# A graph-attention layer and a masked attention layer on 64 graphs: a software pipeline five steps deep replaced by one of twelve steps

## The reference, cut

```python
h = jnp.maximum(_layernorm(x), 0.0)
xl = (h @ W1).reshape(B, N, 4, 128)
e = leaky_relu(asrc[:, :, None, :] + adst[:, None, :, :], 0.2)     # asrc, adst: xl times att_src, att_dst
attn = softmax(where(mask, e, -1e9), axis=1)
h = elu(einsum('bsdh,bshf->bdhf', attn, xl) + b1)
x = x + gat_layer(h, W2, ...)                                      # the same with one head
h = jnp.maximum(_layernorm(x), 0.0)
scores = where(adj, einsum('bhnd,bhmd->bhnm', h @ Wq, h @ Wk) / sqrt(32), -inf)
x = x + relu(einsum('bhnm,bhmd->bhnd', softmax(scores), h @ Wv)) @ Wo
```

## Time and profile before

| | us |
|---|---|
| median of 3 runs | 1104.64 (1102.05 to 1110.62) |
| the profiled execution, its time | 1103.94 |
| its span, first to last instruction | 1102.4 |
| mean granted TensorE clock in it | 0.924 of full speed |
| busy in the span: TensorE, VectorE, ScalarE, GpSimd | 877, 680, 604, 517 |

### The profile page before, as it was taken

How to read it: one execution, slowest core, us unless ns; L and a number is a source line. 1 busy time by engine, 2 the same in 40 slices (tenths; PEclk the granted TensorE clock), 3 DMA queues, 4 the chain that set the end, 5 groups by cost and what they waited for, 6 DMA issues and landing times.

```text
span 1102.4 us, 25604 instructions
## 1 busy us (share of the span) xinstructions
PE 877.0 (80%) x8776; PEld 672.6 (61%) x8776; DVE 680.0 (62%) x2015; ACT 603.7 (55%) x1865; POOL 517.1 (47%) x733
## 2 busy tenths in 40 slices
PE   1277888888888888888888888888888888888884
PEld 0155666666666666666666666666666666666652
DVE  5245667666766666666666666666666666666652
ACT  0245566556666565656555565556565565656541
POOL 3334455445544554455445544544454454445422
PEclk9587999899999998999899899989998998999885
DMA  5001223233322332133122323322431333222122
GB/s 147 0 9 32 58 64 63 38 58 63 64 46 50 64 64 53 42 63 64 42 55 63 59 42 58 64 53 42 64 63 37 59 63 51 45 64 63 38 36 53
DMA packets 165967, 59.45 MB, mean 54 GB/s; under 512 B 138448, under 2 KB 165456, under 8 KB 165840
## 3 DMA queue, kind: packets, MB, share of 16 engines
q1 hardware_dynamic: 165840, 57.83, 27.2%
HBM read 15.86 MB, written 8.39 MB: 22 GB/s over the span
## 4 chain that ended last, share of the span: by engine, by line
PE 59%; DVE 23%; issue 8%; ACT 5%; DMA 2%; POOL 2%; SPq 1%; DVEq 0%; POOLq 0%; ACTq 0%
PE bank L693 21%; PE bank L707 10%; PE bank L832 8%; DVE top L641 7%; PE bank L788 5%; DVE qkT L612 4%; ACT qkT L410 3%; DVE att L587 2%; PE bank L778 2%; DVE x L625 2%; DVE hT L519 2%; PE bank L824 2%; PE bank L719 2%; DMA e3T<-e_split 1%; PE bank L733 1%
## 5 line engine op out<-in xcount | busy, mean ns | idle before, releaser
L319 POOL TENSOR_TENSOR rstd<-var,minus_half 128x1 f32<-128x1 f32 x128 | 71.4, 558 | 300.1 <-DVE var L537 293.2
L420 ACT ACTIVATE e<-bank,nmx,q_power 128x128 f32<-128x128 f32 x512 | 192.6, 471 | 0.0
L307 POOL TENSOR_TENSOR e_split<-e,e_split 128x512 f16<-128x512 f32 x128 | 148.1, 1157 | 10.3
L641 DVE TENSOR_REDUCE top<-bank 128x8 f32<-128x1024 f32 x64 | 78.3, 1224 | 88.3 <-PE bank L788 88.3
L707 PE MATMUL bank<-w,h1T 128*128 128x258 f32 x512 | 127.1, 391 | 0.7 <-DVE h1T L557 0.7
L358 ACT ACTIVATE lr<-bank,power 128x512 f32<-128x512 f32 x64 | 44.0, 688 | 139.3 <-PE bank L744 139.3
L693 PE MATMUL bank<-w_split,hT 128*128 128x260 f16 x768 | 103.5, 288 | 18.2 <-DVE w_split L487 14.7
L297 POOL TENSOR_TENSOR eTn<-eT,rs 128x512 f32<-128x512 f32 x64 | 66.5, 1040 | 108.6 <-DVE rs L637 108.6
L832 PE MATMUL bank<-en,xl 128*128 128x128 f32 x512 | 97.8, 351 | 20.3 <-DVE x L625 18.3
L371 ACT ACTIVATE eT<-lr,nmx 128x128 f32<-128x128 f32 x256 | 98.9, 394 | 18.3 <-DVE nmx L602 18.3
L832 PEld LDWEIGHTS bank<-en,xl 128*128 128x128 f32 x512 | 84.2, 249 | 35.3 <-issue 31.4
(11 more groups left out here) (118 smaller groups left out, 2047.1 us busy)
## 6 DMA issues: line engine op xcount, KB each, us to landing
x_in<-in_x_dram SPq DMA_DIRECT2D x64, 128.0 KB, 2.4
out_dram<-x_out SPq DMA_DIRECT2D x64, 128.0 KB, 1.7
adj_in<-in_adj_dram SPq DMA_DIRECT2D x64, 64.0 KB, 2.1
e3T<-e_split SPq DMA_TRANSPOSE x128, 3.1
w<-in_L_gnn_W_dram SPq DMA_DIRECT2D x2, 256.0 KB, 3.1
w<-in_L_gnn_W_dram SPq DMA_DIRECT2D x1, 512.0 KB, 6.5
att<-in_L_gnn_att_src_dram SPq DMA_DIRECT2D x1, 256.0 KB, 5.1
att<-in_L_gnn_att_dst_dram SPq DMA_DIRECT2D x1, 256.0 KB, 5.7
```

The costliest lines, as they stand in the source:

```text
L307: pool.tensor_tensor(e3_split[:, g.two, half, 1], e, e3_split[:, g.two, half, 0], ALU.subtract).then_inc(s[low_set], 1)
L319: pool.tensor_tensor(rstd[:, g.two, which:which + 1], var[:, g.two, which:which + 1], minus_half[:, :], ALU.pow).then_inc(s[rstd_set], 1)
L420: ins = act.activation(e3[:, g.two, h, :], S[:, h // 4, (h % 4) * N:(h % 4 + 1) * N], ACT.Exp, bias=nmx3[:, g.two, h:h + 1], scale=q_power ...
L641: dve.tensor_reduce(top3[:, g.two, :], S.rearrange("p b (h n) -> p (b h) n", h=4), AX.X, ALU.max, negate=True).then_inc(s["top3_set"], 1)
```

## The change

Every function becomes an item of its own with a lag of 0 to 11 in place of a phase, so that a graph is spread over twelve steps and a full step has twelve graphs in flight; 75 steps do the 64 graphs. Nearly every function keeps its instructions. What is new:
- the order of the items on all five engines, and the lags;
- the eight banks are dealt out anew: Z (bank 7) and Z2 (bank 6) share with S; ABT, O1, T3 and WO share bank 0; ET and AV bank 1; T1, ET2 and O2 bank 3; XL, V, T2 and QK banks 4 and 5; X2 has bank 2 alone;
- x_in, x1 and the masks have rings of eight; load is split in load_adj (lag 2) and load_x (lag 0), and only x of graph 0 is loaded ahead of the weights;
- the mask matmul of scores1, that of scores3, the variance of both norms, ab_high, ab_low, and ab2_evac are items of their own; the sums of W2 run at the first project2;
- `after` and `at_ends` are waits for the readers of a bank: `after` in every step, `at_ends` in the first and last twelve graphs only;
- the preparation of the weights moves from steps 1 to 4 to steps 5 to 8.

The diff, cut to its core:

```diff
-P_, A_, B_, C_, D_ = range(5)
-L_ = -1
+LAGS = 12
...
+def after(eng, sem, g, lag):
+
+    wait(eng, sem, min(g.n + lag + 1, g.count))
+
+
+def at_ends(eng, sem, g, lag):
+
+    if g.n < LAGS or g.n >= g.count - LAGS:
+        after(eng, sem, g, lag)
...
+        x_in = sb("x_in", [128, 8, D])
...
+        mask_gat = sb("mask_gat", [128, 8, N], BF16)
+        mask_mha = sb("mask_mha", [128, 8, N], BF16)
...
-        XL, X2, AV, Z2, Z = bank[:, 0:2, :], bank[:, 4], bank[:, 5], bank[:, 6], bank[:, 7]
-        QK, ET2, T3, V, O2, S = bank[:, 0], bank[:, 4], bank[:, 5], bank[:, 1], bank[:, 6], bank[:, 2:4, :]
-        ABT = bank[:, 5, 0:N // 2].bitcast(F16)
-        T2, ET, WO, T1, O1 = bank[:, 7], bank[:, 7], bank[:, 5], bank[:, 0], bank[:, 6]
+        XL = bank[:, 4:6, :]
+        T1 = bank[:, 3]
+        ABT = bank[:, 0, 0:N // 2].bitcast(F16)
+        Z = bank[:, 7]
+        ET = bank[:, 1]
+        O1 = bank[:, 0]
+        X2 = bank[:, 2]
+        Z2 = bank[:, 6]
+        ET2 = bank[:, 3]
+        O2 = bank[:, 3]
+        T2 = bank[:, 5]
+        QK = bank[:, 5]
+        V = bank[:, 4]
+        S = bank[:, 6:8, :]
+        AV = bank[:, 1]
+        T3 = bank[:, 0]
+        WO = bank[:, 0]
...
-            def load(g):
-                free(sp, s["x1_set"], g, 4)
-                sp.dma_start(x_in[:, g.four, :], x[g.n]).then_inc(x_here[g.four], 16)
+            def load_x(g):
+                if g.n == 0:
+                    return
+                free(sp, s["x1_set"], g, 8)
+                sp.dma_start(x_in[:, g.eight, :], x[g.n]).then_inc(x_here[g.eight], 16)
+
+            def load_adj(g):
...
-            steps(lambda graphs: run([(e3_transpose_first, D_), (load, L_), (e3_transpose_last, D_), (store, D_)], graphs))
+            steps(lambda graphs: run([
+                (e3_transpose_first, 10), (e3_transpose_last, 10), (load_adj, 2), (load_x, 0), (store, 11),
+            ], graphs))
...
-                free(pool, s["av_done"], g)
+                wait(pool, e3T_here[2 * half + g.two], g.dma2 - 16)
...
+            def masks(g):
+
+                pool.wait_ge(adj_here[g.four], g.dma)
+                free(pool, s["zsc_done"], g, 8)
+                free(pool, s["zsc2_done"], g, 8)
+                free(pool, s["s_mask"], g, 8)
+                free(pool, s["masks_set"], g, 2)
...
-                (e3_last_halves, D_), (diagonal2, B_), (rsqrt1, P_), (masks, P_), (normalise, A_), (rsqrt2, B_), (e3_first_halves, C_),
-            ], graphs), before={1: products_w2, 2: lambda: (split_low(0), split_low(1)), 3: lambda: split_low(2), 4: lambda: split_low(3)})
+                (e3_last_halves, 10), (rsqrt1, 3), (masks, 4), (rsqrt2, 8), (normalise, 6), (diagonal2, 7),
+                (e3_first_halves, 9),
+            ], graphs), before={5: lambda: (products_w1(), products_w2()), 6: lambda: (split_low(0), split_low(1)), 7: lambda: split_low(2), 8: lambda: split_low(3)})
...
-                (elu_exp, B_), (mha_exp_last, D_), (relu2, C_), (abT_copy, A_), (gat1_leaky, A_), (qk_copy, C_), (gat2_leaky, B_),
-                (gat1_exp, A_), (gat2_exp, B_), (v_copy, C_), (gat2_copy, B_), (relu1, P_), (gat1_copy, A_), (att_copy, D_),
-                (mha_exp_first, C_),
-            ], graphs), before={
-                1: lambda: act.wait_ge(s["power_set"], 2), 2: lambda: (split_high(0), split_high(1)),
-                3: lambda: (split_high(2), act.wait_ge(s["q_power_set"], 3)), 4: lambda: split_high(3),
-            })
+                (v_copy, 10), (abT_copy, 6), (gat2_leaky, 8), (gat1_copy, 7), (gat2_exp, 8), (qk_copy, 9), (gat1_leaky, 6),
+                (gat2_copy, 8), (elu_exp, 7), (gat1_exp, 6), (att_copy, 11), (mha_exp_first, 9), (mha_exp_last, 9), (relu2, 8),
+                (relu1, 4),
+            ], graphs), before={6: lambda: (split_high(0), split_high(1)), 7: lambda: split_high(2), 8: lambda: split_high(3)})
...
+            def sums_w2():
...
+            def variance(g, which, mv_set, var_set, free_sem):
                 done(dve, s[mv_set], g)
+                free(dve, s[free_sem], g)
                 dve.tensor_scalar(var[:, g.two, which:which + 1], mv[:, g.two, which, 1:2], EPS, None, ALU.add).then_inc(s[var_set], 1)
...
-                dve.wait_ge(x_here[g.four], g.dma)
-                moments(g, 0, x_in[:, g.four, :], "stats_set", "mv_set", "var_set")
+                dve.wait_ge(x_here[g.eight], g.dma8)
+                free(dve, s["z_set"], g)
+                moments(g, 0, x_in[:, g.eight, :], "stats_set", "mv_set")
...
+            def ab_high(g):
+                if g.n == 0:
+                    dve.wait_ge(s["ab_zero"], 1)
                 done(dve, s["xl_done"], g)
                 free(dve, s["abt_done"], g)
-                ab = XL[:, :, HF // 2:HALF]
-                ab_high, ab_low = (ab_split[:, g.two, 2 * H * n:2 * H * (n + 1)].rearrange("p (a c) -> p a c", a=2) for n in range(2))
-                dve.tensor_copy(ab_high, ab).then_inc(s["ab_high"], 1)
+                dve.tensor_copy(ab_part(g, 0), XL[:, :, HF // 2:HALF]).then_inc(s["ab_high"], 1)
+
+            def ab_low(g):
                 done(dve, s["ab_high"], g)
-                dve.tensor_tensor(ab_low, ab, ab_high, ALU.subtract).then_inc(s["ab_set"], 1)
+                dve.tensor_tensor(ab_part(g, 1), XL[:, :, HF // 2:HALF], ab_part(g, 0), ALU.subtract).then_inc(s["ab_set"], 1)
...
+            def ab2_evac(g):
+                if g.n == 0:
+                    sums_w2()
+                done(dve, s["x2_done"], g)
+                free(dve, s["diag2_set"], g)
+                free(dve, s["lr2_set"], g)
+                dve.tensor_tensor(ab2[:, g.two, :], X2[:, D:D + 2], shift2[:, :], ALU.subtract).then_inc(s["ab2_set"], 1)
...
-                (elu, B_), (xl_evac, A_), (relu2_low, C_), (norm1_moments, P_), (xl2_evac, B_), (norm1_apply, P_), (gat1_scores, A_),
-                (qk_low, C_), (gat2_scores, B_), (gat1_recip, A_), (mha_max, C_), (v_low, C_), (relu1_low, P_), (att_norm, D_),
-                (gat2_recip, B_), (residual1, B_), (norm2_moments, B_), (att_low, D_), (norm2_apply, B_), (residual2, D_),
-            ], graphs), before={1: lambda: (prepare_w1(), prepare_b1(), dve.wait_ge(s["ab_zero"], 1)), 2: prepare_w2})
+                (relu1_low, 5), (v_low, 10), (xl2_evac, 8), (norm1_apply, 4), (gat2_scores, 8), (norm1_moments, 2),
+                (gat2_recip, 8), (qk_low, 9), (variance1, 2), (gat1_scores, 6), (elu, 7), (residual1, 8), (mha_max, 9),
+                (norm2_moments, 8), (ab_high, 5), (variance2, 8), (gat1_recip, 6), (att_low, 11), (ab_low, 5), (xl_evac, 5),
+                (norm2_apply, 8), (ab2_evac, 7), (att_norm, 10), (residual2, 11), (relu2_low, 8),
+            ], graphs), before={5: lambda: (prepare_w1(), prepare_b1()), 6: prepare_w2})
...
-            first_waits = {
-                0: lambda: pe.wait_ge(s["ident_set"], 5),
-                1: lambda: (pe.wait_ge(s["w1_low"], 2 * KD), pe.wait_ge(s["pick_set"], 5)),
-                2: w2_ready,
-                3: lambda: pe.wait_ge(s["split_low"], 3),
-                4: lambda: pe.wait_ge(s["split_low"], 4),
-            }
...
             def project1(g):
+                if g.n == 0:
+                    pe.wait_ge(s["w1_low"], 2 * KD)
                 done(pe, s["hT_set"], g)
-                free(pe, s["vv_set"], g, 3)
+                after(pe, s["vv_set"], g, -5)
+                after(pe, s["qkT_set"], g, -4)
+                at_ends(pe, s["ab_set"], g, -1)
+                at_ends(pe, s["xl_set"], g, -1)
...
             def project2(g):
                 done(pe, s["h1T_set"], g)
+                after(pe, s["ab2_set"], g, -1)
+                after(pe, s["xl2_set"], g, -1)
+                if g.n == 0:
+                    w2_sums()
...
             def mha_av(g):
-                pe.wait_ge(e3T_here[g.four], g.dma * 2)
+                pe.wait_ge(e3T_here[g.two], g.dma2)
+                pe.wait_ge(e3T_here[2 + g.two], g.dma2)
                 done(pe, s["vv_set"], g)
-                free(pe, s["x_out_set"], g, 1)
-                wait(pe, s["abT_set"], min(g.n + 4, G))
+                after(pe, s["en_set"], g, 3)
+                at_ends(pe, s["att_set"], g, -1)
...
+            def scores1_mask(g):
+
+                done(pe, s["masks_set"], g)
+                after(pe, s["e3_last"], g, -4)
+                at_ends(pe, s["lr_set"], g, -1)
+                pe.matmul(Z.rearrange("p (h n) -> p h n", h=H), mask_gat[:, g.eight, :], ident16[:, :].unsqueeze(1).to_broadcast((128, H, N)),
+                          start=True, stop=False).then_inc(s["zmask_done"], 1)
...
             def scores3_mask(g):
-                wide = mask_mha[:, g.four, :].unsqueeze(1).to_broadcast((128, 4, N))
+                done(pe, s["masks_set"], g)
+                after(pe, s["lr2_set"], g, 1)
+                after(pe, s["lr_set"], g, 3)
+                at_ends(pe, s["e3_last"], g, -1)
```

(14 more changed lines are left out.)

148 lines of the change are left out of this document (106 added, 42 removed).

## The result

| | before | changed |
|---|---|---|
| median, us | 1103.5 (1102.05 to 1110.62) | 830.61 (829.5 to 831.13) |
| span of the profiled execution, us | 1102.4 | 828.7 |
| granted clock, mean of the span | 0.924 | 0.978 |
| ratio of the times | | 0.752, 95% interval 0.748 to 0.755 |

The changed kernel is faster by a quarter. The forecast was 853 us and its direction was right; the time came out beside that of the rival *Nothing interferes* (833 us, chance 0.22), and the forecast's own step was too long.

The account below looks back on a forecast made before the run. The prediction took TensorE's waits for returns from other engines, not a full engine, to bound the kernel. Ramp 102 + 58 steps x 12.05 + drain 50 = 851 us of span, +2 gives 853 us; range 820 to 945.

Parts of the forecast that it names:

- Nothing interferes: Rival: every checked wait has slack, so a steady step takes 11.7 us and the total is 833 us; chance 0.22.
- What bounds the kernel: Steady step before: TensorE needs 11.75 us and waits 3.5 us for returns from other engines; no engine is full.
- The walk: New steady step laid out in TensorE order, each return checked against when it is wanted; all five stops go, leaving 11.7 us.
- the tightest place: Shared Z and S bank, first half: gat1_leaky ends at 3.8 us, scores3_mask wants it at 3.9; 0.1 us left.
- The second place: Shared bank, second half: exponentials done at 11.0 us, next scores1_mask wants that at 11.7; 0.7 us left.
- The added waits: Extra TensorE waits name things done long before, so cost nothing; 1.0 us a step kept for the range.
- TensorE's occupancy: Start-to-start times of TensorE's items in the new steady step, summing to 11.7 us without stops.
- What I add, 0.35 us a step,: norm1_apply on VectorE held up beside e3_last_halves on GpSimd, bounds 0 and about 1.0 us, delaying TensorE; 12.05 us a step.
- The step of 12.4 to 12.7 us: Steady step if VectorE and GpSimd instructions exclude each other entirely, delaying norm1_apply by some 0.7 to 1.0 us.
- The clock: Granted clock at 1.00 throughout the full steps, worth 0.6 us a step.
- The ramp: Start, about 102 us until the first full step: prepare_w1 waits for moments of graphs 1 and 2, +7.5 us.
- The drain: End, behind the full steps: the last steps losing items and the last graph's chain, together 50 us.

Follow-up runs that it names:

- Run 2: The kernel before with the four transposes of transpose1 done twice into the same bank: 1067.36 us, ratio 0.965.
- run 4: The changed kernel with normalise ahead of rsqrt2 in GpSimd's order: 835.20 us.
- run 3: The changed kernel with the third float16 product left out in project1, qk, project_v and project_out, so less precise: 807.06 us.
- run 5: The changed kernel with x of graphs 1 and 2 also loaded ahead of the weights: 830.63 us.
- the fastest kernel: The changed kernel with x[1], x[2] and adj[0] loaded ahead of the weights and one all-reduce instead of two: 812.79 us.
- run 6: The changed kernel with x[1], x[2] and adj[0] loaded ahead of the weights: 823.15 us.

## Why the prediction was right, and where it was off

- **What bounds the kernel** held. The reading was 3.5 us of stops a step and 11.75 us of TensorE's own. Run 2 shows that the returns set it (0.44 us more work, no longer a step), the changed kernel that the rest is 11.54 to 11.65.
- **The walk** held in its times nearly to the tenth, but not in what it called left over. At the tightest place it reckoned 0.05 us for the handing over and found 0.1 us of room; the handing over from gat1_leaky to scores3_mask takes 0.14 us, and the room there is nil. That cost some 0.02 us a step. The second place came out at 0.7 us as said.
- **The added waits** were costed at nothing, with 1.0 us a step kept for the range. They cost 0.11 us in 18 of the 58 steps, 2 us in all: the one that stands behind gat1_leaky's wait in scores3_mask. No other item of TensorE starts later in these steps, so the other `at_ends` waits cost nothing there; what the waits of `after` cost, which stand in every step, no run shows apart.
- **TensorE's occupancy** was written 0.125 us too long (11.7 against 11.575), 7 us in 58 steps. The terms that were too large: project2, which runs from 399.89 to 401.64, takes 1.75 us for the 1.80 written, mha_av 0.61 for 0.7, aggregate1 0.95 for 1.0; the rest is rounding both ways, and 0.03 us the other way for the waits just named.
- **What I add, 0.35 us a step,** is the step that failed: nothing of it reached TensorE, which is 20 us. I took the middle of 0 and 1.0 us. Two things were wrong. First, norm1_apply did fall beside e3_last_halves, at 1.30 us as said, but GpSimd ran 0.3 us later than placed:

```profile
405.29 0.40 DVE L597 TENSOR_SCALAR z<-x_in,mv,rstd 128x256 f32<-128x256 f32 x1
405.46 1.24 POOL L343 TENSOR_TENSOR e_split<-e,e_split 128x512 f16<-128x512 f32 x1
```

  norm1_apply started 0.17 us ahead of the remainder, and it was the remainder that grew (1.24 instead of 1.16 us). On VectorE the hold-up fell on norm2_apply, which starts behind normalise (700 ns instead of 413); in the step shown it ends at 402.47 and norm2_transpose, which reads it, starts at 403.12, 0.65 us later. Second, the whole delay was charged to the place with the least slack, though qk_copy in between waits for qk anyway and covers about 0.2 us of it: in run 4 norm1_apply is 0.23 us longer and gat1_leaky 0.01 us later. The path itself exists: in run 3, where norm1_apply ends 0.58 us later, 0.36 us of that arrive at gat1_leaky. That norm1_apply was spared in the changed kernel is luck of 0.2 us between two queues.
- **How long the hold-up is.** Of the norm applies of all runs here 861 took over 480 ns, and 858 of them ended 0.14 to 0.15 us behind the GpSimd instruction beside them, however much of that was still to run (rows of 0.70, 0.76 and 1.12 us alike). By full exclusion norm2_apply would have begun its 0.41 us at 402.33, where normalise ends, and ended at 402.74; it ended at 402.47. The Trainium skill (SBUF — State Buffer, section "Who interferes with whom") speaks of exclusion for the whole instruction, where VectorE's is in a 2-port mode; whether a norm apply ran in one, no run shows. This trace agrees in that the later one ends behind the earlier one, and differs in the size, 0.15 us for 0.41. The step of 12.4 to 12.7 us that was worked out by that rule did not come. The prediction's remark that the trace of before has only the brief kind of overlap was not quite so: its two longest norm applies (678 and 677 ns) ran for 0.53 us beside a cast that had started 0.08 us ahead.
- **The clock** held: 1.00 for all 58 steps. Run 2 measured its worth by itself, 0.57 us a step where 0.6 was said. VectorE is busy 87% of these steps (583.59 of 671.40 us), where 85% or more was said.
- **The ramp's** sum was right (step 11 at 102.65 where 102 was said; prepare_w1 at 19.64, second all-reduce to 45.5, GpSimd's next at 52.57 for 19, 46 and 52.3). Its cause was half of it: adj[0] arrives as late as x[1] and x[2], and run 5 shows that to mend one alone brings nothing.
- **The drain** took 54.7 us instead of 50. The last exponentials end at 811.59 + 2.90 = 814.5, 40.5 us behind the end of the last full step (774.0) where 37.4 were said, and 14.2 us remain behind them where 13.0 were.
- **The sum** of the misses: 0.6 - 58 x 0.475 + 4.7 = -22 us, which is the difference of 853 and 831. That the rival *Nothing interferes* comes within 2 us of the measured time is partly luck: its step was 7 us too long in all and its drain 4.7 us too short, and something does interfere.

## What to carry to other kernels

If an engine is busy 80% and stops several times in each step for an answer to what it has just handed over, write down the start-to-start occupancies of its items: their sum was, in this kernel, the step that the deeper pipeline reached to within 0.1 us, with every return walked through beforehand. Count the handing over in that walk (0.05 to 0.14 us here) and put the wait that ends last behind all others (argued from these rows, not tried): a further wait executed behind it cost 0.11 us. Equal times on TensorE and on a return mean that less work for TensorE alone will gain little (run 3). Mending one return alone moves part of its stop to the next. Charge a contention to the path only where the place of both instructions is known better than the slack; and look in the new ramp for every load that the new order wants early, not for the first one found.

## What the runs showed of the hardware

- Work added to an engine that stops often made the kernel faster: 0.44 us of transposes more a step, 1067 us instead of 1105, as the granted clock stayed at the 2.4 GHz level (1.00 instead of 0.95 over 58 steps).
- A VectorE tensor_scalar on 128x256 float32 of 414 ns takes 700 ns in the median, at most 1121, where a GpSimd tensor_tensor on 128x512 float32 that started before it runs beside it; it ends 0.15 us behind that one. Where VectorE's started first, by 0.17 us, it kept its 405 ns and the GpSimd instruction took 1.24 instead of 1.16 us. Not every GpSimd instruction holds it up: in the kernel before, norm1_apply kept 411 to 414 ns beside the first instruction of the masks (128x128, int32 in), which had started 0.06 us ahead and ran on past its end.
- A matmul with three waits (scores3_mask) starts 0.14 us behind the end of the ScalarE instruction for which it waits last (gat1_leaky). With a fourth wait behind that one it starts 0.25 us behind it, though what the fourth asks for was done about 1 us before.
- An all-reduce over partitions of 0.4 us costs GpSimd 6 us before and 7 us behind it. The 6 us are not seen where GpSimd had been idle for over 10 us: there it starts 0.13 us behind the end of VectorE's maxima in the fastest kernel (22.61, above) and 1.7 us behind it in run 6 (20.38 against 18.69).
